# A fused four-layer kernel on one core: last halves of two products, gate order and one base product rearranged

## What is computed

```python
x = x + L0_ffn(L0_cond(x, len0))   # long convolution along tokens; fp8 linear 512x512
x = x + L1_ffn(L1_cond(x, ids))    # linear picked per sequence; NF4-quantized gated MLP, hidden 1376
x = x + L2_ffn(L2_cond(x, lang))   # base linear + top-2 of 8 low-rank experts; memory of 128 slots
x = x + L3_ffn(L3_cond(x, len3))   # gate from a 5-tap convolution of means; linear + gated rank 32
```

```python
# L1_ffn, last step
return einsum('bsh,dh->bsd', silu(gate) * up, dq3)
# L2_ffn: softmax over the top 8 of 128 slots, times a gate of each token
w = softmax(attn)                               # exp, then divided by its sum
aux_out = (w @ sel_vals) @ Wvd.T @ Wvu.T
u = clip(norm_var * 0.5 + sigmoid(learned) * 2.5, 0, 5)
gate = sigmoid(gate_w1 * u_norm + gate_bias); gate = where(gate < 0.05, 0, gate)
return hidden_states + gate * aux_out
# L3_cond: x * sigmoid(conv(mean of x over each sequence))
# L3_ffn
H = x @ W.T + b
z = x @ A                                       # rank 32
weights = probs * sigmoid((probs - thresh) / 0.5); weights /= sum
return H + ((z * (weights @ LiMEs)) @ Bmat) * scaling
```

## Time and profile before

| | us |
|---|---|
| runs before | 900.28, 904.56, 902.46 |
| median | 902.46 |
| profiled execution, whole | 904.57 |
| its span, first to last instruction | 902.7 |
| PE busy | 857.8 (95%) |
| DVE busy | 616.6 (68%) |
| ACT busy | 410.2 (45%) |
| POOL busy | 156.3 (17%) |

### The profile page before, as it was taken

One profiled execution on the slowest core, in us unless ns is written; L12 is line 12 of the kernel. 1 busy time (PEld: TensorE's weight loads), 2 busy tenths in 40 slices (PEclk: granted clock), 3 DMA queues, 4 the chain that ended last, 5 costly groups with the idle time before them and its releaser, 6 DMA issues.

```text
span 902.7 us, 10586 instructions
## 1 busy us (share of the span) xinstructions
PE 857.8 (95%) x3265; PEld 458.5 (51%) x3266; DVE 616.6 (68%) x958; ACT 410.2 (45%) x530; POOL 156.3 (17%) x174
## 2 busy tenths in 40 slices
PE   0599999999999999999999999999999999989998
PEld 0496448998444444444344444444444555443342
DVE  7799997887888889899998844253452353257624
ACT  5124647886787776877878520000012132143000
POOL 5200008900121111222102210002402021020000
PEclk9999999999999999999999999999999999999999
DMA  6796138650000001101000110013010000002112
GB/s 184 245 336 232 58 117 283 200 215 28 23 24 24 0 18 32 33 0 33 32 1 0 41 49 1 0 61 126 15 51 1 1 0 1 1 1 46 47 46 93
DMA packets 34728, 60.97 MB, mean 68 GB/s; under 512 B 6040, under 2 KB 8424, under 8 KB 34040
## 3 DMA queue, kind: packets, MB, share of 16 engines
q1 hardware_dynamic: 33896, 60.26, 19.5%
q0 software_dynamic: 704, 0.10, 0.3%
q10 hardware_dynamic: 80, 0.01, 0.0%
HBM read 50.84 MB, written 8.47 MB: 66 GB/s over the span
## 4 chain that ended last, share of the span: by engine, by line
PE 91%; DVE 3%; issue 2%; POOL 2%; ACT 1%; DMA 0%; SPq 0%; POOLq 0%; ACTq 0%; DVEq 0%
PE ps L931 89%; PE ps L989 1%; PE ps L1252 1%; DVE acc L1534 1%; DVE W2T L1395 1%; DMA T<-kpad 0%; PE ps L1286 0%; POOL lan_i L650 0%; ACT Yp L868 0%; DVE Yp L1547 0%; PE ps L1209 0%; ACT W1T L895 0%; SPq L534 0%; POOL gsc L645 0%; POOL kk L645 0%
## 5 line engine op out<-in xcount | busy, mean ns | idle before, releaser
L749 ACT ACTIVATE above<-raw,cst 128x1024 bf16<-128x1024 f32 (+2 forms) x225 | 271.9, 1233 | 120.3 <-DVE acc L1534 44.2
L1534 DVE SCALAR_TENSOR_TENSOR acc<-above,acc 128x1024 f32<-128x1024 bf16 (+2 forms) x112 | 151.4, 1352 | 25.5 <-ACT above L749 21.5
L931 PE MATMUL ps<-Yp,W3T 128*128 (+1 forms) x740 | 159.3, 370 | 3.0 <-DVE Yp L1547 1.6
L931 PE MATMUL ps<-Up,W2T 128*128 128x512 f32 (+1 forms) x404 | 160.6, 593 | 0.0
L931 PE MATMUL ps<-Up,W1T 128*128 128x512 f32 x344 | 155.4, 594 | 0.1
L1534 DVE SCALAR_TENSOR_TENSOR T<-above,T 128x1024 f32<-128x1024 bf16 (+1 forms) x84 | 118.1, 1406 | 22.4 <-ACT above L749 19.3
L931 PEld LDWEIGHTS ps<-Yp,W3T 128*128 128x128 f32 x740 | 102.3, 191 | 55.1 <-issue 52.6
L931 PEld LDWEIGHTS ps<-Up,W2T 128*128 128x128 f32 (+1 forms) x404 | 66.5, 177 | 85.9 <-issue 85.9
L931 PEld LDWEIGHTS ps<-Up,W1T 128*128 128x128 f32 x344 | 64.3, 190 | 79.1 <-issue 76.3
L931 PE MATMUL ps<-X,W3T 128*128 128x512 f32 (+1 forms) x176 | 79.0, 602 | 0.0
L931 PE MATMUL ps<-X,W2T 128*128 128x512 f32 x140 | 61.3, 594 | 0.0
(11 more groups left out here) (337 smaller groups left out, 885.0 us busy)
## 6 DMA issues: line engine op xcount, KB each, us to landing
W3T<-in_wa SPq DMA_DIRECT2D x8, 1024.0 KB, 5.4
raw<-in_w SPq DMA_DIRECT2D x20, 256.0 KB, 3.0
W3T<-kpad SPq DMA_DIRECT2D x9, 512.0 KB, 7.3
Up<-in_xconv SPq DMA_DIRECT2D x4, 1024.0 KB, 12.0
X<-in_xT SPq DMA_DIRECT2D x4, 1024.0 KB, 9.1
W1T<-in_wa SPq DMA_DIRECT2D x4, 1024.0 KB, 5.8
xkeep<-X SPq DMA_DIRECT2D x4, 1024.0 KB, 4.7
X<-xkeep SPq DMA_DIRECT2D x4, 1024.0 KB, 8.9
```

The source lines that it names most:

```text
L749: nc.scalar.activation(above[0:h, m % 2, 0:w], raw[0:h, u % 2, 0:w], ACT.Relu, scale=STEEP, bias=cst[0:h, C_BND + i:C_BND + i + 1]).then_i ...
L931: return nc.tensor.matmul(o, l, r, start=start, stop=stop, **kw)
L1534: V.scalar_tensor_tensor(out=ac, in0=src, scalar=float(STEPS[i]), in1=ac, op0=ALU.min, op1=ALU.add).then_inc(s["m_used"], 1)
```

## The change

1. The last Strassen product (kind "4", round 1, `o` = 1) is done in two column halves of 256, the second in bank 4 (`BANK1["7"]`). A new semaphore `p_4h` tells DVE of the first; it adds 8 sequences after each.
2. At the last block ACT does its exponentials as 0, tanh twice, 1, gate tanh, 2, 3. DVE makes the denominators and gates of the first 12 tiles and their three products first, then those of the last four.
3. DVE makes the gates' diagonal (`gex`) before adds 0 and 1 and not after them.
4. `base(4)` comes before the first lift.
5. The last output tile (15) is done in two column halves, each base and lift, in banks 1 and 2; DVE and SP take each half by itself (`p_oh`; the last transfer is two of 128 KB).

```diff
+        col_halves = [slice(0, TW // 2), slice(TW // 2, TW)]
+        LAST_BANKS = [BANKS3[-1], BANKS3[0]]
...
             for n in range(TB * DC):
                 tb, oc = n // DC, n % DC
-                sp.wait_ge(s["d_o"], n + 1)
-                sp.dma_start(out[oc * P:(oc + 1) * P, tok(tb)], results[n]).then_inc(s["l_out"], 16)
-            sp.wait_ge(s["l_out"], 16 * TB * DC)
+                for i, part in enumerate(col_halves if n == TB * DC - 1 else [slice(0, TW)]):
+                    sp.wait_ge(s["d_o"], n + 1 + i)
+                    sp.dma_start(out[oc * P:(oc + 1) * P, tb * TW + part.start:tb * TW + part.stop], results[n][:, part]
+                                 ).then_inc(s["l_out"], 16)
+            sp.wait_ge(s["l_out"], 16 * (TB * DC + 1))
...
                 else:
+                    act.wait_ge(s["d_am"], TB)
+                    probs(0)
                     act.wait_ge(s["a_lr"], TB - 1)
                     nc.scalar.activation(gq[:, 0, 0:TT - NT], lrn[:, 0:TT - NT], ACT.Tanh, scale=0.5, bias=gsc[:, 3:4])
                     act.wait_ge(s["p_lr"], TB)
                     nc.scalar.activation(gq[:, 0, TT - NT:], ps[:, 5, 0:NT], ACT.Tanh, scale=0.5, bias=gsc[:, 3:4]
                                          ).then_inc(s["a_sg"], 1)
...
-            act.wait_ge(s["d_un"], 1)
-            nc.scalar.activation(gq[:, 2, :], gq[:, 1, :], ACT.Tanh, scale=gsc[:, 4:5], bias=gsc[:, 5:6]
-                                 ).then_inc(s["a_gt"], 1)
+                if tb < TB - 1:
+                    act.wait_ge(s["d_am"], tb + 1)
+                    for t in range(NT):
+                        probs(t)
+                else:
+                    probs(1)
+                    act.wait_ge(s["d_un"], 1)
+                    nc.scalar.activation(gq[:, 2, :], gq[:, 1, :], ACT.Tanh, scale=gsc[:, 4:5], bias=gsc[:, 5:6]
+                                         ).then_inc(s["a_gt"], 1)
+                    probs(2)
+                    probs(3)
...
+                final = (p, kind, o) == (NP - 1, "4", OH - 1)
+                for part in col_halves if final else [slice(0, TW)]:
+                    if part.start:
+                        b = BANK1["7"]
+                    for k, (l, r) in enumerate(terms):
+                        last = mm(ps[:, b, part], l, r[:, part], k == 0, rest is None and k == KH - 1)
...
+                    if part.stop < TW:
+                        last.then_inc(s["p_4h"], 1)
...
+                if n == TB * DC - 1:
+                    pe.wait_ge(s["d_o"], 9)
+                    for part, b in zip(col_halves, LAST_BANKS):
+                        cols = slice(tb * TW + part.start, tb * TW + part.stop)
+                        for c in range(DC):
+                            mm(ps[:, b, part], l3w[:, c, oc * P:(oc + 1) * P], X[:, c, cols], c == 0, False)
+                        mm(ps[:, b, part], bm4[g, :], zq[g, cols], False, True).then_inc(s["p_oh"], 1)
+                    return
...
             for half in range(2):
                 ranks(half)
+            base(4)
             pe.wait_ge(s["l_bm"], 16 * DC)
-            last_base = 3
+            last_base = 4
...
+                if o == OH - 1:
+                    dve.wait_ge(s["p_4h"], 1)
+                    add_back(TB - 2, *seqs, range(0, n // 2))
+                    dve.wait_ge(s["p_down"], done_step(1, "4", o))
+                    add_back(TB - 2, seqs[0], ps[:, BANK1["7"]:BANK1["7"] + 1, :], range(n // 2, n))
...
+            dve.wait_ge(s["a_pr"], TT - NT)
+            twice_den(early)
             dve.wait_ge(s["a_sg"], 1)
             stt(gq[:, 1, :], gq[:, 0, :], 1.25, gq[:, 1, :], ALU.mult, ALU.add)
             V.tensor_scalar(gq[:, 1, :], gq[:, 1, :], 0.5, 2.0, ALU.max, ALU.min).then_inc(s["d_un"], 1)
+            dve.wait_ge(s["a_gt"], 1)
+            gated(early)
+            for tb in range(TB - 1):
+                gate_probs(tb)
             dve.wait_ge(s["a_pr"], TT)
...
+            twice_den(late)
+            gated(late)
+            gate_probs(TB - 1)
...
-            add_aux(range(0, 2))
             dve.wait_ge(s["a_yg"], 1)
...
-            add_aux(range(2, 8))
+            add_aux(range(0, 8))
...
+                if n == TB * DC - 1:
+                    for i, part in enumerate(col_halves):
+                        cols = slice(tb * TW + part.start, tb * TW + part.stop)
+                        dve.wait_ge(s["p_oh"], i + 1)
+                        tt(tmp[n % 2][:, part], ps[:, LAST_BANKS[i], part], G[:, cols], ALU.mult)
+                        V.scalar_tensor_tensor(out=results[n][:, part], in0=tmp[n % 2][:, part], scalar=b3[:, oc:oc + 1],
+                                               in1=X[:, oc, cols], op0=ALU.add, op1=ALU.add).then_inc(s["d_o"], 1)
+                    continue
```

More of the change, by code:

```diff
@@ L863, in _, with probs @@
             for tb in range(TB):
+                def probs(t):
+                    k = tb * NT + t
+                    nc.scalar.activation(PR[:, k, :], am[:, t, :], ACT.Exp, bias=nmx[:, t:t + 1],
+                                         accum_out=den[:, k:k + 1]).then_inc(s["a_pr"], 1)
                 if tb + 1 < TB:
@@ L1115, in step @@
                 b = BANK1[kind] + o
[L1116 to L1120, removed]
+                final = (p, kind, o) == (NP - 1, "4", OH - 1)
[4 more added lines that the diff above has]
+                        last = mm(ps[:, b, part], l, r[:, part], k == 0, rest is None and k == KH - 1)
+                    if rest:
+                        cols, tb = rest
+                        last = mm(ps[:, b, part], W3T[0:HCH[-1], NH - 1, cols], H[tb, NH - 1][0:HCH[-1], part], False, True)
+                    if part.stop < TW:
+                        last.then_inc(s["p_4h"], 1)
                 last.then_inc(s["p_down"], 1)
@@ L1650, in load_places, with add_back @@
                 places[tb] = [dve.value_load(order[0:1, tb * n + i:tb * n + i + 1], min_val=0, max_val=NB - 1) for i in range(n)]
-            def add_back(tb, ocs, src):
-                for i, b in enumerate(places[tb]):
+            def add_back(tb, ocs, src, some=range(TW // S)):
+                for i in some:
+                    b = places[tb][i]
                     dve.tensor_tensor(X[:, ocs, bass.ds(b * S, S)], X[:, ocs, bass.ds(b * S, S)],
@@ L1834, in _, with twice_den, gated, gate_probs @@
             ts(gq[:, 1, :], lv[:, :], lvs[:, 1:2], 1.25, ALU.mult, ALU.add)
+            early, late = slice(0, TT - NT), slice(TT - NT, TT)
+            def twice_den(some):
+                ts(gq[:, 3, some], den[:, some], 2.0, None, ALU.mult, ALU.bypass)
+                link(V.reciprocal(gq[:, 3, some], gq[:, 3, some]))
+            def gated(some):
+                stt(gq[:, 3, some], gq[:, 2, some], 1.0, gq[:, 3, some], ALU.add, ALU.mult)
+                stt(gq[:, 4, some], gq[:, 2, some], 2 * 0.05 - 1.0, gq[:, 3, some], ALU.is_ge, ALU.mult)
+            def gate_probs(tb):
+                tl = slice(tb * NT, (tb + 1) * NT)
+                V.tensor_tensor(PR[:, tl, :], PR[:, tl, :], gq[:, 4, tl].unsqueeze(2).to_broadcast([P, NT, NSLOT]),
+                                ALU.mult).then_inc(s["d_pn"], 1)
+            dve.wait_ge(s["a_pr"], TT - NT)
+            twice_den(early)
             dve.wait_ge(s["a_sg"], 1)
@@ L1837, in _ @@
             V.tensor_scalar(gq[:, 1, :], gq[:, 1, :], 0.5, 2.0, ALU.max, ALU.min).then_inc(s["d_un"], 1)
+            dve.wait_ge(s["a_gt"], 1)
+            gated(early)
+            for tb in range(TB - 1):
+                gate_probs(tb)
             dve.wait_ge(s["a_pr"], TT)
-            ts(gq[:, 3, :], den[:, :], 2.0, None, ALU.mult, ALU.bypass)
-            link(V.reciprocal(gq[:, 3, :], gq[:, 3, :]))
-            dve.wait_ge(s["a_gt"], 1)
-            stt(gq[:, 3, :], gq[:, 2, :], 1.0, gq[:, 3, :], ALU.add, ALU.mult)
-            stt(gq[:, 4, :], gq[:, 2, :], 2 * 0.05 - 1.0, gq[:, 3, :], ALU.is_ge, ALU.mult)
-            for tb in range(TB):
-                tl = slice(tb * NT, (tb + 1) * NT)
-                V.tensor_tensor(PR[:, tl, :], PR[:, tl, :], gq[:, 4, tl].unsqueeze(2).to_broadcast([P, NT, NSLOT]),
-                                ALU.mult).then_inc(s["d_pn"], 1)
+            twice_den(late)
+            gated(late)
+            gate_probs(TB - 1)
             def add_aux(some):
```

16 lines of the change are left out of this document (8 added, 8 removed).

## The result

| | before | after |
|---|---|---|
| median of 5 runs, us | 904.15 (900.28 to 906.59) | 896.76 (896.05 to 897.49) |
| ratio | | 0.9914, 95% interval 0.9894 to 0.9935 |
| profiled execution, us | 904.57 | 897.49 |
| its span, us | 902.7 | 895.7 |
| mean granted clock | 0.993 | 1.000 |

The forecast was 896.0, with a range of 893.0 to 900.2. By the medians the kernel became faster by 7.4 us (0.8%); the ratio, measured on the runs together, says 0.86%.

What follows compares the result with a forecast made beforehand. TensorE (PE) was taken to set the pace, with 91% of the span. Idle and tail of 4.4 us plus clock of 3.1 made 7.5: 897.1 from 904.57, 895.0 from the median 902.46; forecast 896.0, range 893 to 900.2.

Steps and rivals of the forecast that it cites:

- Part A: Last Strassen product in column halves: PE's 0.74 us idle before the first logits goes, gain 0.7 us.
- Rival 3: Weight loads of the 256-column instructions are not hidden: 8.4 us more, 903.4 us in all; chance 0.03.
- Part B: Exponentials among the tanh at the last block: PE's idle before the turned probabilities goes entirely, gain 2.2 us.
- rival 2: Each switch between exp and tanh brings a table load, a loss of about 1.5 us: 901.1 us; chance 0.05.
- Part C: Gates' diagonal before two adds: first spread earlier, second spread later, a loss of 0.3 us.
- Part D: Base product 4 before the first lift covers PE's wait there wholly, gain 0.94 us.
- Part E: Last output tile in halves: DVE's last steps and the last transfer get shorter, gain 0.9 us.
- PE's 0.05: Last output tile: PE's extra cost for 20 instructions of 256 columns instead of 10 of 512, taken as 0.05 us.
- The clock: Granted clock stays up at the turnings and the lifts once the idles before them are gone, gain 3.1 us.
- the first fall: Fall of the granted clock over the logits: left where it is, since the logits are small too.
- The sum: Whole kernel: 4.4 us of idle and tail plus 3.1 of clock, 7.5 us gained.
- rivals 1: Clock does not come back: only 4.4 us are left, 898.1 us, or 899.7 with a new fall; chance 0.26.

Runs made afterwards that it cites:

- fit_pad: Changed kernel with adds 0 and 1 moved into DVE's waits and 16 tiny VectorE memory sets before the first gates: 896.17 us.
- u_gex: Changed kernel with the gates' diagonal put back behind adds 0 and 1: 896.73 us.
- u_base4: Changed kernel with base product 4 put back behind the first four lifts: 897.85 us.
- exp_filled: Changed kernel with the old order of exponentials and gates put back and two useless 512-column matmuls in PE's idle before the turnings: 898.82 us.
- fit_uneven: As fit_pad, with the last output tile split into 384 and 128 columns in place of 256 and 256: 894.81 us.

## Why the prediction was right, and where it was not

The time was right, 896.0 for 896.76, and so was the kind of account: idle of PE removed, plus clock. By its steps:

- **Part A**, 0.7: measured 0.78. The halves cost 0.22 an instruction (5.28 us in place of the 5.25 from 656.44 to 661.69), the values' small matmuls took 0.07 less, the adds of the first are hidden, and PE itself is next, as said. Rival 3, weight loads that are not hidden, did not occur.
- **Part B**, 2.2: measured 1.70, and an idle of 0.55 where the prediction allowed 0.3. The mechanism held, as ScalarE's timeline in the kernel after shows:
```profile
799.06 1.28 ACT L871 ACT_TABLE_LOAD   x1
800.35 0.40 ACT L871 ACTIVATE W1T<-Up 128x128 f32<-128x128 f32 x1
...
800.75 0.29 ACT L898 ACTIVATE gq<-lrn,gsc 128x12 f32<-128x12 f32 x1
```

There is one table load between gelu and exponentials and none among them and the tanh, so the loads of rival 2 did not come; the exponential starts 0.01 after the load ended. The drain of about 1.38 us that the Trainium skill (ScalarE: Activation LUTs, What ACT_TABLE_LOAD costs) adds to a load does not show here either. Block 3 was no hindrance. The term was mis-sized by a pause of 0.40 on DVE that no step of the sum had; `fit_pad` took it away and 0.36 of the idle with it. The 0.19 that stayed is unexplained.
- **Part C**, -0.3: measured -0.42, and `u_gex` confirms it. The loss was foreseen because the second spread was counted in adds.
- **Part D**, 0.94: measured 0.81 without the clock. The bases, now in two groups, took 0.20 longer (3.63 and 10.50 against 13.93 in `u_base4`), the same price as at the changes of part E, and the rank products 0.07 less to the next start. The clock's share at this place was 1.65, as taken; yet `u_base4` alone showed no fall in six executions. To put that share down to part D's idle alone was too simple: it came back only together with the two other idles.
- **Part E**, 0.9: measured 0.64. DVE (0.53 for 0.56) and transfer (0.52 for 0.4) were near; the step that failed is PE's 0.05, which was 0.41, since the price from the earlier trace rows holds for matmuls of the same rows in a run and not for the change between 128 and 32 rows.
- **The clock**, 3.1: 4.4 between the two profiles, 4.6 between the groups of the kernel before (905.0 and 900.4). The sizes of the two falls that I counted were right (1.29 for 1.4, 1.65 for 1.65). The step that failed is that the first fall would stay because the logits are small: it went too (1.43).
- **The sum**, 7.5 against the profiled execution: 7.9 by stages, 7.1 by the times. 3.6 us of the gain are there even against executions without a fall (900.4 to 896.8; 4.4 forecast), and the rest only against executions with falls. The 2.1 us between the profiled execution and the median, which I left open, are such a difference: the three runs shown, 900.28, 902.46 and 904.56, lie by their times in the three groups. So too large an idle part and too small a clock part met at the right total, and that was luck. The forecast and its rivals also did not start from one number: 896.0 lies between a sum from 904.57 and one from 902.46, rival 2 is counted from 896.0, rivals 1 and 3 from 902.46, which sets them up to 1 us apart.

The three idles explain the falls as far as this: with them filled or gone the clock stood at 0.999 or more in all executions of the kernel after, and of `exp_filled`, `fit_pad` and `fit_uneven`; with all three back it fell at least twice in each of ten, by the mean clock. Which of them brings a fall in a given execution is not settled. By the Trainium skill (TensorE: Matmul & The Clock Gate, What's actually happening), the watch on activity is free-running and the point of a change differs from run to run. These runs agree with it so far, since the same code gave three groups. No run shows the cause itself.

## What to carry to other kernels

Where PE sets the pace, look for idles even of under 1 us and add to each what the granted clock does behind it; read the mean clock of all executions before taking one profile's falls for the rule, and leave out of it the time after the last matmul. Before work is moved forward on a helping engine, ask in what unit PE's later waits are counted: the diagonal moved forward won 0.8 at one wait and lost 1.2 at the next, and fitting the adds into waits that were there won 1.1. When a last tile is split to shorten the tail, count the changes between kinds of matmul that the split doubles.

## What was not expected of the hardware

- With useless matmuls in an idle of 2.24 us no execution of ten had a lowered mean clock; without them four of eight had, on another chip. In the profiles the work behind took no longer (240.1 and 240.0 us).
- The granted clock was at 0.50 in three stretches of a kernel in which PE never idled longer than 2.3 us since product 4, and one idle of 0.94 us was followed by such a stretch in some executions and not in others.
- VectorE paused 0.40 us with nothing to wait for, in the same step of all profiles of the new order, and not once 16 instructions stood ahead of it; a like pause of 0.40 stood among the adds to `X` before the change.
- Each change between the base matmuls of 128 rows and the lifts of 32 rows took about 0.2 us.
